# A gated cross-attention stack on one core: first key weights requested first, context rounded in three pieces, GpSimd's power behind the first weight rounding, keys of batch 1 last

## The chip, the cores and the metric

The kernel runs on 1 core of one Trainium2 chip. The metric is device time in microseconds, median over the runs. The profiled execution is a single one; its span runs from its first to its last instruction.

## What is computed

Four layers of a gated cross-attention model on x (2 x 256 x 512) with a context (2 x 512 x 512). Each layer adds a gated attention and a gated MLP to x, each behind a layer norm. The change is in the opening of the first attention, which is, cut to what matters:

```
def _L0_xattn_ref(latents, context, Wq, Wk, Wv, Wo):      # 32 heads, 4 key/value heads, head dim 128
    hidden_states = jnp.concatenate([context, latents], axis=1)
    q = (latents @ Wq).reshape(b, q_len, N_KV_HEADS, N_GROUPS, HEAD_DIM)
    k = (hidden_states @ Wk).reshape(b, kv_len, N_KV_HEADS, HEAD_DIM)
    v = (hidden_states @ Wv).reshape(b, kv_len, N_KV_HEADS, HEAD_DIM)
    scores = jnp.einsum('bqhgd,bkhd->bhgqk', q, k) * scale
    attn = jax.nn.softmax(scores.astype(jnp.float32), axis=-1).astype(q.dtype)
    out = jnp.einsum('bhgqk,bkhd->bqhgd', attn, v)
    return out.reshape(b, q_len, N_HEADS * HEAD_DIM) @ Wo

x = x + jnp.tanh(g_xattn[0]) * _L0_xattn_ref(_layernorm(x, axis=-1), ctx_4096, ...)
x = x + jnp.tanh(g_ffn[0]) * _L0_ffn_ref(_layernorm(x, axis=-1), ...)
...                                                       # layers 1 to 3 alike
```

## The kernel before

Each engine runs a program of its own, written out by hand, and waits on semaphores. Nothing is scheduled at run time: what stands first on an engine runs first.

**Products in three parts.** To multiply in float32 accuracy, every operand is kept as a rounded part (HI) and the rest (LO), and each product is three passes: HI by HI, HI by LO, LO by HI (`PAIRS`). So a weight or a context tile can be used only when both parts exist. Weights are split by GpSimd in `att_pool` (L526 writes HI, L529 writes LO). The context, 512 rows by 1024 columns in `ctxraw`, is split by ScalarE (HI, L1899) and VectorE (LO, L1934), one batch (4 x 512 columns per partition) at a time; `ctx_split` counts the finished pieces. The transposed latents `xT` are split out of PSUM by ScalarE (L419) and VectorE (L425).

**The jobs.** The attention's small products are jobs. ("K", u, c) projects the keys of key head u: c = 0 and 1 are the context of batch 0 and 1, c = 2 the latents of both. ("Q", h, 0) projects a head's queries, ("V", u, c) six tiles of values, ("O", h, r) the output rows. A K or Q job is 12 matmuls of 512 columns (L560, L583). Below, K0, K1, K2 and Q0 mean the four jobs of `self.first`. ScalarE and VectorE take every job's result out of PSUM in the order of `place`, and scores(n) (L614) is the first step of the main loop: 128 items of scores, softmax, transpose and weighted values, with jobs between them. TensorE is in order, so that whatever delays scores(0) delays all behind it.

**The opening, before.** SyncE requests, in this order: the context of batch 0 (1 MB), x (1 MB), the context of batch 1 (1 MB), the gates, the key weights (256 KB), and then the stream of `att_sp`: the weights of query heads 0 and 1 and, behind the latter, the MLP's `worg`, `fwq`, `fkeys` (`mlp0_early_sp`). From the third entry on, the stream's request j waits for the split of entry j - 2. GpSimd splits the key weights and both query weights, and then computes rstd as a power of the variances (`ln_first_pool`, L382). VectorE has by then taken the statistics (L340 to L345) and waits for rstd to write the normalised rows (L348); TensorE transposes them (L399).

The place of `ctxraw` in memory overlaps the output weights before the change (its group begins with a filler `kept0` of 12 x 512 words), so GpSimd waits for the second context split before it goes on to the value weights.

Of the kernel before, what the change touches and what calls it, by code (L numbers as in the profile page):

```python
# [15 lines left out]
F32 = mybir.dt.float32  # L16
# [53 lines left out]
class Attention:  # L70
# [7 lines left out]
    def __init__(self, tag, heads, kv, hd, tiles, first_tile, before):  # L78
        self.tag, self.heads, self.kv, self.hd = tag, heads, kv, hd
        self.g = heads // kv  # L80
        self.items = RT * heads
        self.pairs = self.items // 2
        self.scale = float(hd) ** -0.5
        inner, last = {}, {}
        for h in range(heads):
            n = RT * h
            if h + 1 < heads:
                last[n + 1] = ("Q", h + 1, 0)
            last[n + 6], last[n + 7], last[n + 8], inner[n + 9] = [("O", h, r) for r in range(RT)]
        for u in range(1, kv):  # L90
            n = RT * self.g * u
            inner[n - 2], inner[n - 1], inner[n] = ("K", u, 0), ("K", u, 2), ("K", u, 1)
        for u in range(0, kv, 2):
            n, v, h = RT * self.g * u, [("V", u, c) for c in range(6)], self.g * u - 1
            if u == 0:
                last[0], inner[2], last[2], inner[3], last[3], inner[4] = v
            else:
                inner[n + 2], last[n + 2], inner[n + 3], inner[n + 4], last[n + 4], inner[n + 5] = v
                last[n + 3], inner[n + 6], last[n + 6], inner[n + 7] = [("O", h, r) for r in range(RT)]
                last[n + 7], inner[n + 8], last[n + 8], inner[n + 9] = [("O", h + 1, r) for r in range(RT)]  # L100

        self.tail = [("O", heads - 1, 2), ("O", heads - 1, 3)]
        for at in (inner, last):
            for n in [n for n, job in at.items() if job in self.tail]:
                del at[n]
        self.steps = [(n, inner.get(n), last.get(n)) for n in range(self.items + 4)]
        self.first = [("K", 0, 0), ("K", 0, 1), ("K", 0, 2), ("Q", 0, 0)]
        order = self.first + [j for _, *both in self.steps for j in both if j] + self.tail
        self.place = {j: i + 1 for i, j in enumerate(order)}
        assert len(self.place) == len(order) == 3 * kv + 3 * kv + heads + RT * heads  # L110
        self.bank = {j: 7 for j in order}
        for c in range(3):
            self.bank["K", 0, c] = c
        for c in (0, 1, 3):
            self.bank["V", 0, c] = 6
        self.bank[self.tail[0]], self.bank[self.tail[1]] = 3, 6
        self.free, used = {}, {}
        for j in order[3:-2]:
            self.free[j] = used.get(self.bank[j], 0)
            used[self.bank[j]] = self.place[j]  # L120
        self.hi_place = {j: i + 1 for i, j in enumerate(j for j in order if j[0] != "O")}


        need = [(RT * h - 3, 0, ("q", h, 0)) for h in range(heads)] + [(RT * h + 6, 1, ("o", h, 0)) for h in range(heads)]
        need += [(RT * self.g * u - 3, 1, ("k", u, 0)) for u in range(kv)]
        need += [(RT * self.g * u + 2, p, ("v", u, p)) for u in range(0, kv, 2) for p in range(2)]
        self.stream = [e for *_, e in sorted(need)]
        a, b = self.stream.index(("k", 0, 0)), self.stream.index(("q", 0, 0))
        self.stream[a], self.stream[b] = self.stream[b], self.stream[a]
        self.split = {e: i + 1 for i, e in enumerate(self.stream)}  # L130

        self.amax_at, self.scale_at, self.step_at, self.load_before, self.round_after, self.store_before = (
            {} for _ in range(6))
        for i, h in enumerate(tiles):
            n = first_tile + i
            self.amax_at[RT * h + 1], self.scale_at[RT * h + 5], self.step_at[RT * h + 9] = n, n, n
            self.load_before["q", h + 2, 0], self.round_after["o", h + 2, 0], self.store_before["o", h + 4, 0] = n, n, n
        self.stored = first_tile + len(tiles)

        J, E = len(order), len(self.stream)  # L140
        count = {"raw0": 8 * E, "raw1": 8 * E, "split_hi": E, "split": E, "w_full": J, "w": J,
                 "w_hi": len(self.hi_place), "rden": heads}
        count.update({n: self.items for n in ("scores", "nmax", "exps", "turned", "pT_hi", "pT")})
        count.update({n: self.pairs for n in ("pv", "oT_hi", "oT")})
        self.before = before.after if before else dict.fromkeys(count, 0)
        self.after = {n: self.before[n] + count[n] for n in count}
# [6 lines left out]
def build(nc, t, out):  # L153
    with ExitStack() as ctx:
# [75 lines left out]
            values_of = {A0: vv0, A1: vv1}  # L230

        with ExitStack() as grp:
            sb("kept0", [P, 12, 512], F32, grp)
            ctxraw = sb("ctxraw", [P, KT, B * CTX], F32, grp)


# [76 lines left out]
        with ExitStack() as grp:  # L313
# [6 lines left out]
            x8 = sb("x8", [P, D], F8, grp)  # L320
            hq = sb("hq", [P, 2, FPAD], BF16, grp)
            hqT = sb("hqT", [P, FT, P], BF16, grp)

        block = ctx.enter_context(nc.Block())

# [118 lines left out]
        def att_sp(sp, A, u, between=None):  # L444
# [18 lines left out]
            for j, entry in enumerate(A.stream):  # L463
# [12 lines left out]
                else:  # L476
                    att_wait(sp, A, "split", 0)
                to, arrived = raw[:, j % 2, :], sem(f"att_raw{j % 2}")
                if w == "k":
                    sp.dma_start(to[:, 0:KT * A.hd], t[f"{A.tag}_wk"][h]).then_inc(arrived, 16)  # L480
                elif w == "v":
                    n = KT * A.hd
# [11 lines left out]
        def att_pool(g, A, layer_norm):  # L494
# [15 lines left out]
            for j, entry in enumerate(A.stream):  # L510
# [23 lines left out]
                    att2_split_pool(g, l2wkv, l2wkv_raw, "l2_wkv", 1)  # L534
                if A is A1 and entry == ("o", 13, 0):
                    att2_split_pool(g, l2wq, l2wq_raw, "l2_wq", 2)
                if j == 2:
                    layer_norm()

        def values_tile(A, part, pair, c):  # L540
# [4 lines left out]
        def att_pe(pe, A, u):  # L545
# [6 lines left out]
            def job(what):  # L552
                kind, h, c = what
                b = A.bank[what]
                if kind == "K":
                    wait("split", A.split["k", h, 0])
                    for k in range(KT):
                        for wp, xp in PAIRS:
                            rhs = ctxT[:, xp, k, c * CTX:(c + 1) * CTX] if c < B else xT[:, xp, k, :]
                            last = nc.tensor.matmul(bank(b, 512, hd), wk[:, wp, k * hd:(k + 1) * hd], rhs,  # L560
# [39 lines left out]
            def scores(n):  # L600
# [2 lines left out]
                if r == 0:  # L603
                    wait("w", A.place["Q", h, 0])
                if n % (RT * A.g) == 0:
                    wait("w", A.place["K", group, 2])
                if n % (RT * A.g) == 2:
                    wait("w", A.place["K", group, 1])
                if n >= 2:
# [35 lines left out]
                    last.then_inc(sem("att_pv"), 1)  # L645

            if A is A0:
                pe.wait_ge(sem("ctx_split"), 1)
                job(A.first[0])
                turn_pe(pe, u)  # L650
                pe.wait_ge(sem("ctx_split"), 2)
                job(A.first[1])
            else:
                job(A.first[0])
                job(A.first[1])
                turn_pe(pe, u)
            pe.wait_ge(sem("xT_lo"), (u // 2 + 1) * RT)
            job(A.first[2])
            job(A.first[3])
            for n, inner, end in A.steps:  # L660
                if n < A.items:
                    scores(n)
# [1173 lines left out]
        @block.sync  # L1836
        def _(sp):
            context = t["ctxT"].rearrange("(k p) n -> p k n", p=P)
            sp.dma_start(ctxraw[:, :, 0:CTX], context[:, :, 0:CTX]).then_inc(sem("ctx_loaded0"), 16)
            sp.dma_start(x[:], t["x"].rearrange("(r p) d -> p r d", p=P)).then_inc(sem("x_loaded"), 16)  # L1840
            sp.dma_start(ctxraw[:, :, CTX:B * CTX], context[:, :, CTX:B * CTX]).then_inc(sem("ctx_loaded1"), 16)
# [15 lines left out]
        def _(g):  # L1857
# [3 lines left out]
            g.wait_ge(sem("const"), 3)  # L1861
            nc.gpsimd.affine_select(out=ident[:], in_=ident[:], compare_op=ALU.not_equal, fill=1.0, base=0,
                                    pattern=[[-1, P]], channel_multiplier=1).then_inc(sem("const"), 1)
            def before_output_weights():
                ln_first_pool(g)
                g.wait_ge(sem("ctx_split"), 2)

            att_pool(g, A0, before_output_weights)
            ln_pool(g, 1)
            mlp0_pool(g)  # L1870
            att_pool(g, A1, lambda: ln_pool(g, 2))
# [22 lines left out]

        @block.scalar
        def _(a):
            for b in range(B):
                a.wait_ge(sem(f"ctx_loaded{b}"), 16)
                nc.scalar.activation(ctxT[:, HI, :, b * CTX:(b + 1) * CTX], ctxraw[:, :, b * CTX:(b + 1) * CTX],  # L1899
                                     ACT.Copy).then_inc(sem("ctx_hi"), 1)  # L1900
            a.wait_ge(sem("gates_loaded"), 16)
            nc.scalar.activation(tg[:], gates[:], ACT.Tanh).then_inc(sem("gates_ready"), 1)
            turn_act(a, 0)
            att_act(a, A0, 0)
            a.wait_ge(sem("w3_stored"), 32 * A0.stored)
            turn_act(a, 1, plain=True)
# [21 lines left out]

        @block.vector
        def _(v):  # L1930
            def split_context(b):
                cols = slice(b * CTX, (b + 1) * CTX)
                v.wait_ge(sem("ctx_hi"), b + 1)
                nc.vector.tensor_tensor(ctxT[:, LO, :, cols], ctxraw[:, :, cols], ctxT[:, HI, :, cols].bitcast(F32),  # L1934
                                        ALU.subtract).then_inc(sem("ctx_split"), 1)

            split_context(0)
            ln_first_dve(v)
            split_context(1)
            turn_dve(v, 0)  # L1940
            v.wait_ge(sem("gates_ready"), 1)
            v.wait_ge(sem("ctx_split"), 2)
            att_dve(v, A0, 0)
            mlp0_dve(v)
            turn_dve(v, 2)
# [95 lines left out]
```

## Time and profile before

| | |
|---|---|
| median of 3 runs | 1447.77 us (1447.07 to 1454.72) |
| profiled execution, device time | 1453.91 us |
| its span | 1452.2 us |
| TensorE busy | 1362.6 us, 94% of the span |
| VectorE, ScalarE, GpSimd busy | 945.3, 588.6, 475.1 us |
| mean granted TensorE clock | 0.969 |

Device time is 1.71 us more than the span. In the page's slices all but the first show TensorE at seven tenths busy or more; the first slice, 36 us long, shows it at four tenths. Idle time of an engine that nobody waits for costs nothing. The granted clock is 1.00 at 2.4 GHz and 0.50 at 1.2 GHz.

### The profile page before, as it was taken

The page shows a single profiled execution, that of the slowest core. Times are in us where ns is not written, and L with a number is a line of the kernel's source. Part 1 is how long each engine was busy: PE and PEld are TensorE (multiplying, and loading weights), DVE is VectorE, ACT ScalarE, POOL GpSimd, SP SyncE. Part 2 cuts the span into 40 slices and gives each one's busy share as a digit, 9 for nine tenths or more (in the row PEclk, how much of TensorE's full clock was granted, in tenths as well). Part 3 has the DMA queues.
Part 4 walks back from the last instruction along what each step waited for, and adds up shares of the span by engine and source line. Part 5 has one row for each costly group of instructions (what it writes and reads, how often), then busy time and mean ns, then how long its engine had stood idle before and what let it go on. Part 6 is the DMA issues. An engine that isn't in the chain of part 4 may idle for free.

```text
span 1452.2 us, 21125 instructions
## 1 busy us (share of the span) xinstructions
PE 1362.6 (94%) x8219; PEld 1081.1 (74%) x8219; DVE 945.3 (65%) x1375; ACT 588.6 (41%) x1012; POOL 475.1 (33%) x359
## 2 busy tenths in 40 slices
PE   4999999999999999989999999999899999899766
PEld 3989889988889889964788888888774444577422
DVE  4488778864688688762466864767656673352596
ACT  2444444443344344430244443444344677222112
POOL 4226435361235525411321671235213002144100
PEclk9999999999999999999999999999997899999888
DMA  5111111021012111011111111002012000461000
GB/s 174 51 53 47 52 47 60 26 70 37 23 52 77 34 51 48 19 47 39 55 33 38 39 37 41 28 17 67 1 50 77 1 1 1 143 168 44 1 1 29
DMA packets 54337, 68.19 MB, mean 47 GB/s; under 512 B 26416, under 2 KB 34896, under 8 KB 54240
## 3 DMA queue, kind: packets, MB, share of 16 engines
q1 hardware_dynamic: 54240, 66.84, 15.3%
q8 instruction: 67, 1.10, 0.3%
q14 instruction: 30, 0.25, 0.1%
HBM read 57.13 MB, written 5.37 MB: 43 GB/s over the span
## 4 chain that ended last, share of the span: by engine, by line
PE 84%; DVE 9%; ACT 3%; issue 2%; DMA 1%; POOL 0%; SPq 0%; POOLq 0%; ACTq 0%; DVEq 0%
PE ps L639 13%; PE ps L614 12%; PE ps L590 9%; PE ps L623 9%; PE ps L583 8%; PE ps L575 5%; PE ps L560 5%; PE ps L1496 4%; PE ps L1124 3%; PE ps L1150 3%; PE ps L1509 2%; PE ps L1106 1%; PE ps L1135 1%; PE ps L862 1%; PE ps L869 1%
## 5 line engine op out<-in xcount | busy, mean ns | idle before, releaser
L708 ACT ACTIVATE pT<-ps 128x768 fp32r<-128x768 f32 x192 | 156.0, 812 | 288.7 <-PE ps L623 287.1
L639 PE MATMUL ps<-pT,vv 128*128 128x256 f32 (+1 forms) x1728 | 251.3, 290 | 2.5 <-DVE oT L818 2.5
L811 DVE TENSOR_TENSOR pT<-ps,pT 128x768 fp32r<-128x768 f32 x192 | 183.7, 957 | 77.9 <-ACT pT L708 77.2
L614 PE MATMUL ps<-kT,qT 128*128 128x512 f32 (+3 forms) x1152 | 231.6, 336 | 2.8 <-DVE qT L763 2.8
L614 PEld LDWEIGHTS ps<-kT,qT 128*128 128x128 f32 (+1 forms) x1152 | 201.5, 188 | 43.9 <-DVE qT L763 3.7
L639 PEld LDWEIGHTS ps<-pT,vv 128*128 128x128 f32 (+1 forms) x1728 | 215.1, 180 | 3.1 <-DVE pT L811 2.9
L716 ACT ACTIVATE prob<-ps,rows_and_turned 128x768 f32<-128x768 f32 x192 | 172.2, 897 | 84.9 <-DVE rows_and_turned L799 84.9
L799 DVE TENSOR_REDUCE rows_and_turned<-ps 128x1 f32<-128x768 f32 x192 | 182.7, 952 | 26.0 <-PE ps L614 25.7
L526 POOL TENSOR_TENSOR wo<-raw,one 128x512 fp32r<-128x512 f32 (+1 forms) x48 | 49.9, 1040 | 395.1 <-PE ps L590 394.6
L590 PE MATMUL ps<-wo,oT 128*128 128x512 f32 (+1 forms) x576 | 169.6, 403 | 5.6 <-DVE qT L763 2.6
L623 PE MATMUL ps<-ident,prob 128*128 128x128 f32 x1152 | 157.1, 272 | 0.4 <-DVE pT L811 0.4
L753 DVE SCALAR_TENSOR_TENSOR x<-ps,rows_and_turned,x 128x512 f32<-128x512 f32 x192 | 143.1, 745 | 7.2 <-PE ps L590 7.2
L583 PE MATMUL ps<-xT,wq 128*128 128x512 f32 (+1 forms) x576 | 142.2, 395 | 0.0
L623 PEld LDWEIGHTS ps<-ident,prob 128*128 128x128 f32 x1152 | 132.3, 140 | 11.0 <-ACT prob L716 1.3
L583 PEld LDWEIGHTS ps<-xT,wq 128*128 128x128 f32 (+1 forms) x576 | 100.2, 179 | 26.3
L590 PEld LDWEIGHTS ps<-wo,oT 128*128 128x128 f32 (+1 forms) x576 | 94.9, 189 | 18.7 <-DVE qT L763 4.4
L1340 DVE TENSOR_REDUCE qrow<-ps 128x1 f32<-128x512 f32 x128 | 83.3, 687 | 38.1 <-PE ps L1124 37.0
L1436 POOL TENSOR_TENSOR f2w<-f2raw,f2w 128x1024 fp32r<-128x1024 f32 (+1 forms) x22 | 43.1, 1964 | 182.8 <-ACT f2w L1540 181.7
L526 POOL TENSOR_TENSOR wq<-raw,one 128x512 fp32r<-128x512 f32 (+1 forms) x48 | 46.9, 976 | 106.9 <-PE ps L583 103.5
L1306 ACT ACTIVATE prob<-ps 128x1024 f32<-128x1024 f32 x64 | 65.4, 1025 | 29.0 <-PE ps L1135 28.7
L560 PE MATMUL ps<-ctxT,wk 128*128 128x512 f32 (+1 forms) x192 | 50.5, 414 | 18.4 <-POOL wk L529 15.2
L387 POOL TENSOR_TENSOR rstd<-vare,neghalf 128x1 f32<-128x1 f32 x28 | 20.9, 746 | 139.1 <-DVE vare L364 139.1
(227 smaller groups left out, 1908.5 us busy)
## 6 DMA issues: line engine op xcount, KB each, us to landing
f2raw<-in_f_w SPq DMA_DIRECT2D x11, 776.0 KB, 4.9
rows_and_turned<-in_m_w SPq DMA_DIRECT2D x11, 768.0 KB, 4.2
raw<-in_l_wq SPq DMA_DIRECT2D x32, 256.0 KB, 2.7
raw<-in_l_wo SPq DMA_DIRECT2D x32, 256.0 KB, 2.7
raw<-in_l_wq SPq DMA_DIRECT2D x16, 192.0 KB, 2.4
raw<-in_l_wo SPq DMA_DIRECT2D x16, 192.0 KB, 2.5
w3gu<-rows_and_turned SPq DMA_DIRECT2D x11, 256.0 KB, 3.2
ctxraw<-in_ctxT SPq DMA_DIRECT2D x2, 1024.0 KB, 7.5
```

The lines of the kernel that those rows point to most:

```text
L526: nc.gpsimd.tensor_tensor(dst[:, HI], src, one[0:src.shape[0], :].to_broadcast(src.shape), ALU.mult).then_inc(sem("att_split_hi"), 1)
L560: last = nc.tensor.matmul(bank(b, 512, hd), wk[:, wp, k * hd:(k + 1) * hd], rhs, start=(k == 0 and (wp, xp) == PAIRS[0]), stop=(k == KT - ...
L583: last = nc.tensor.matmul(bank(b, 512, hd), wq[:, h % 2, wp, k * hd:(k + 1) * hd], xT[:, xp, k, :], start=(k == 0 and (wp, xp) == PAIRS[0] ...
L590: last = nc.tensor.matmul(bank(b), oT[0:hd, h % 2, op, c * P:(c + 1) * P], wo[0:hd, h % 2, wp, :], start=(op, wp) == PAIRS[0], stop=(op, w ...
L614: last = nc.tensor.matmul(sc[:, lo:hi], qT[0:hd, h % 2, qp, r * P:(r + 1) * P], kT[0:hd, kp, b, lo:hi], start=(qp, kp) == PAIRS[0], stop=( ...
L623: last = nc.tensor.transpose(ps[:, 4 + j // 3, (j % 3) * P:(j % 3 + 1) * P], prob[:, m % 3, j * P:(j + 1) * P], ident[:])
L639: last = nc.tensor.matmul(bank(6, 256, hd), vv[:, vp, b * VT + j, group % 2 * hd:(group % 2 + 1) * hd], pT[:, q % 2, pp, j, :], start=(j = ...
L708: nc.scalar.activation(turned_p(m, HI), ps[:, 4:6, 0:S // 2].rearrange("p a (j c) -> p a j c", j=3), ACT.Copy).then_inc(sem("att_pT_hi"), 1)
L716: nc.scalar.activation(prob[:, n % 3, :], sc[:, 0:S], ACT.Exp, bias=nmax[:, n % 32:n % 32 + 1], accum_out=rsum[:, n % 32:n % 32 + 1]).then ...
L753: nc.vector.scalar_tensor_tensor(x[:, c, :], bank(A.bank[what]), rden[:, n:n + 1], x[:, c, :], ALU.mult, ALU.add).then_inc(sem("att_w"), 1)
L799: nc.vector.tensor_reduce(nmax[:, n % 32:n % 32 + 1], sc[:, 0:S], AX.X, ALU.max, negate=True).then_inc(sem("att_nmax"), 1)
L811: nc.vector.tensor_tensor(turned_p(m, LO), ps[:, 4:6, 0:S // 2].rearrange("p a (j c) -> p a j c", j=3), turned_p(m, HI).bitcast(F32), ALU. ...
```

## The change

SyncE requests the key weights ahead of everything. The context is split in three pieces: the first half of batch 0's contraction rows, its second half, and all of batch 1. VectorE splits the third piece behind the split of `xT`, ScalarE's tanh of the gates goes behind its part of `xT`. GpSimd computes rstd directly behind the split of the key weights. TensorE runs K0 (its first half needs the first piece alone), the transposes, K2, Q0, and last K1. `ctxraw` moves up in memory, clear of the output weights.

```diff
         self.first = [("K", 0, 0), ("K", 0, 1), ("K", 0, 2), ("Q", 0, 0)]
+        if before is None:
+            self.first = [("K", 0, 0), ("K", 0, 2), ("Q", 0, 0), ("K", 0, 1)]
...
+        if before is None:
+            self.bank["K", 0, 1] = 5
...
-            sb("kept0", [P, 12, 512], F32, grp)
+            sb("kept0", [P, 31, 512], F32, grp)
...
+        CTX_PARTS = ((0, 0, 2), (0, 2, KT), (1, 0, KT))
...
-                if w == "k":
+                if A is A0 and j == 0:
+                    pass
+                elif w == "k":
...
-                if j == 2:
+                if j == (0 if A is A0 else 2):
                     layer_norm()
...
                     for k in range(KT):
+                        if what == ("K", 0, 0) and A is A0 and k % 2 == 0:
+                            pe.wait_ge(sem("ctx_split"), k // 2 + 1)
...
-                    wait("w", A.place["K", group, 2])
+                    wait("w", max(A.place["K", group, 2], A.place["Q", h, 0]))
...
             if A is A0:
-                pe.wait_ge(sem("ctx_split"), 1)
                 job(A.first[0])
                 turn_pe(pe, u)
-                pe.wait_ge(sem("ctx_split"), 2)
+                pe.wait_ge(sem("xT_lo"), RT)
                 job(A.first[1])
+                job(A.first[2])
+                pe.wait_ge(sem("ctx_split"), 3)
+                job(A.first[3])
...
+            sp.dma_start(raw[:, 0, :], t["l0_wk"][0]).then_inc(sem("att_raw0"), 16)
             sp.dma_start(ctxraw[:, :, 0:CTX], context[:, :, 0:CTX]).then_inc(sem("ctx_loaded0"), 16)
...
-            def before_output_weights():
-                ln_first_pool(g)
-                g.wait_ge(sem("ctx_split"), 2)
-
-            att_pool(g, A0, before_output_weights)
+            att_pool(g, A0, lambda: ln_first_pool(g))
...
-            for b in range(B):
+            for b, lo, hi in CTX_PARTS:
...
+            turn_act(a, 0)
             a.wait_ge(sem("gates_loaded"), 16)
             nc.scalar.activation(tg[:], gates[:], ACT.Tanh).then_inc(sem("gates_ready"), 1)
-            turn_act(a, 0)
...
             split_context(0)
+            split_context(1)
             ln_first_dve(v)
-            split_context(1)
             turn_dve(v, 0)
+            split_context(2)
             v.wait_ge(sem("gates_ready"), 1)
```

GpSimd's first instructions behind its constants, before (wk, wq, wv are the weights of keys, queries and values, raw what was loaded, rstd the power):

```order
L526 TENSOR_TENSOR wk<-raw,one 128x512
L529 TENSOR_TENSOR wk<-raw,wk 128x512
L526 TENSOR_TENSOR wq<-raw,one 128x512
L529 TENSOR_TENSOR wq<-raw,wq 128x512
L526 TENSOR_TENSOR wq<-raw,one 128x512
L529 TENSOR_TENSOR wq<-raw,wq 128x512
L382 TENSOR_TENSOR rstd<-vare,neghalf 128x4
L526 TENSOR_TENSOR wv<-raw,one 128x512
```

The same place on GpSimd after the change:

```order
L534 TENSOR_TENSOR wk<-raw,one 128x512
L537 TENSOR_TENSOR wk<-raw,wk 128x512
L388 TENSOR_TENSOR rstd<-vare,neghalf 128x4
L534 TENSOR_TENSOR wq<-raw,one 128x512
L537 TENSOR_TENSOR wq<-raw,wq 128x512
L534 TENSOR_TENSOR wq<-raw,one 128x512
L537 TENSOR_TENSOR wq<-raw,wq 128x512
L534 TENSOR_TENSOR wv<-raw,one 128x512
```

The power moved ahead of the four instructions that split the query weights of heads 0 and 1, so these four now stand directly behind it.

TensorE's first instructions, before:

```order
L560 MATMUL ps<-ctxT,wk 128x512 x12
L399 MATMUL ps<-ident,rows_and_turned 128x128 x16
L560 MATMUL ps<-ctxT,wk 128x512 x12
L560 MATMUL ps<-xT,wk 128x512 x12
L583 MATMUL ps<-xT,wq 128x512 x12
L614 MATMUL ps<-kT,qT 128x512 x3
```

TensorE's first instructions after the change:

```order
L570 MATMUL ps<-ctxT,wk 128x512 x12
L405 MATMUL ps<-ident,rows_and_turned 128x128 x16
L570 MATMUL ps<-xT,wk 128x512 x12
L593 MATMUL ps<-xT,wq 128x512 x12
L570 MATMUL ps<-ctxT,wk 128x512 x12
L624 MATMUL ps<-kT,qT 128x512 x3
```

The second job on the context (K1) moved from directly behind the transposes to directly ahead of the scores; the number of matmuls is the same.

## Rows read from the trace of the kernel before

**Rows 1.** The page: span, and TensorE's busy time.

```profile
span 1452.2 us, 21125 instructions
PE 1362.6 (94%) x8219; PEld 1081.1 (74%) x8219; DVE 945.3 (65%) x1375; ACT 588.6 (41%) x1012; POOL 475.1 (33%) x359
```

**Rows 2.** Timeline, 0 to 38 us: start, us, engine, line [idle before, releaser].

```profile
5.95 1.91 ACT L1899 ACTIVATE ctxT<-ctxraw 128x2048 fp32r<-128x2048 f32 x1 [3.87 <-DMA ctxraw<-in_ctxT]
7.89 2.29 DVE L1934 TENSOR_TENSOR ctxT<-ctxraw,ctxT 128x2048 fp32r<-128x2048 f32 x1 [7.89 <-ACT ctxT L1899]
10.10 2.47 DVE L340 BATCH_NORM_STATS2 stat<-x 128x6 f32<-128x512 f32 x4
...
13.02 0.77 DVE L345 TENSOR_SCALAR vare<-mv 128x4 f32<-128x4 f32 x1
...
13.84 1.26 POOL L529 TENSOR_TENSOR wk<-raw,wk 128x512 fp32r<-128x512 f32 x1
...
15.25 4.85 PE L560 MATMUL ps<-ctxT,wk 128*128 128x512 f32 x12 [15.25 <-POOL wk L529]
...
20.26 1.03 POOL L382 TENSOR_TENSOR rstd<-vare,neghalf 128x4 f32<-128x4 f32 x1
21.32 1.92 DVE L348 TENSOR_SCALAR rows_and_turned<-x,mv,rstd 128x512 f32<-128x512 f32 x4 [7.54 <-POOL rstd L382]
...
22.02 3.06 PE L399 MATMUL ps<-ident,rows_and_turned 128*128 128x128 f32 x16 [1.92 <-DVE rows_and_turned L348]
...
25.11 0.60 ACT L419 ACTIVATE xT<-ps 128x512 fp32r<-128x512 f32 x1 [0.26 <-PE ps L399]
25.35 2.48 DVE L425 TENSOR_TENSOR xT<-ps,xT 128x512 fp32r<-128x512 f32 x4
...
25.49 3.29 PE L560 MATMUL ps<-ctxT,wk 128*128 128x512 f32 x12 [0.41 <-DVE ctxT L1934]
...
28.62 2.96 PE L560 MATMUL ps<-xT,wk 128*128 128x512 f32 x12
...
31.42 2.96 PE L583 MATMUL ps<-xT,wq 128*128 128x512 f32 x12
...
35.79 1.32 PE L614 MATMUL ps<-kT,qT 128*128 128x512 f32 x6 [1.41 <-DVE qT L763]
```

**Rows 3.** Tiles ctxraw and x, time from request to landing; DMA in one microsecond.

```profile
DMA to landing us min/median/max: 5.1/7.5/9.9
...
DMA to landing us min/median/max: 7.8/7.8/7.8
...
7.00:8.00 1.00, 0.00 (x0) 1.00 1.02 399
```

**Rows 4.** Timeline at 695 us, second attention's layer norm: GpSimd and VectorE.

```profile
695.59 0.78 POOL L387 TENSOR_TENSOR rstd<-vare,neghalf 128x1 f32<-128x1 f32 x1 [2.79 <-DVE vare L364]
696.34 0.82 POOL L526 TENSOR_TENSOR wv<-raw,one 128x384 fp32r<-128x384 f32 x1
696.40 1.04 DVE L368 TENSOR_SCALAR rows_and_turned<-x,mv,rstd 128x512 f32<-128x512 f32 x1 [0.44 <-POOL rstd L387]
```

**Rows 5.** Timeline at 88 us, first attention: GpSimd and VectorE.

```profile
87.57 1.04 POOL L526 TENSOR_TENSOR wq<-raw,one 128x512 fp32r<-128x512 f32 x1 [2.11 <-PE ps L583]
...
88.69 0.19 DVE L773 TENSOR_SCALAR rows_and_turned<-rows_and_turned 128x48 uint32<-128x48 uint32 x1
88.69 1.33 POOL L529 TENSOR_TENSOR wq<-raw,wq 128x512 fp32r<-128x512 f32 x1
88.79 1.28 DVE L775 TENSOR_SCALAR rows_and_turned<-rows_and_turned 128x48 uint32<-128x48 uint32 x1
```

**Rows 6.** Windows of all engines; the clock granted to TensorE stands behind POOL's.

```profile
23.00:25.50 2.50, 2.08 (x11) 1.68 (x9) 2.50 (x3) 1.86 (x4) 0.00 (x0) 0.50 0.00 0
...
26.50:34.00 7.50, 7.50 (x34) 5.99 (x33) 3.32 (x6) 1.20 (x2) 3.64 (x4) 1.00 0.27 70
1104.50:1135.50 31.00, 30.86 (x143) 12.80 (x142) 16.49 (x26) 15.11 (x18) 6.59 (x2) 0.50 0.00 1
```

More of the change, by code:

```diff
@@ L656, in att_pe @@
                 turn_pe(pe, u)
-            pe.wait_ge(sem("xT_lo"), (u // 2 + 1) * RT)
-            job(A.first[2])
-            job(A.first[3])
+                pe.wait_ge(sem("xT_lo"), 2 * RT)
+                job(A.first[2])
+                job(A.first[3])
             for n, inner, end in A.steps:
@@ L1896, in _ @@
         def _(a):
-            for b in range(B):
+            for b, lo, hi in CTX_PARTS:
                 a.wait_ge(sem(f"ctx_loaded{b}"), 16)
-                nc.scalar.activation(ctxT[:, HI, :, b * CTX:(b + 1) * CTX], ctxraw[:, :, b * CTX:(b + 1) * CTX],
+                nc.scalar.activation(ctxT[:, HI, lo:hi, b * CTX:(b + 1) * CTX], ctxraw[:, lo:hi, b * CTX:(b + 1) * CTX],
                                      ACT.Copy).then_inc(sem("ctx_hi"), 1)
+            turn_act(a, 0)
             a.wait_ge(sem("gates_loaded"), 16)
             nc.scalar.activation(tg[:], gates[:], ACT.Tanh).then_inc(sem("gates_ready"), 1)
-            turn_act(a, 0)
             att_act(a, A0, 0)
@@ L1930, in _, with split_context @@
         def _(v):
-            def split_context(b):
+            def split_context(i):
+                b, lo, hi = CTX_PARTS[i]
                 cols = slice(b * CTX, (b + 1) * CTX)
-                v.wait_ge(sem("ctx_hi"), b + 1)
-                nc.vector.tensor_tensor(ctxT[:, LO, :, cols], ctxraw[:, :, cols], ctxT[:, HI, :, cols].bitcast(F32),
+                v.wait_ge(sem("ctx_hi"), i + 1)
+                nc.vector.tensor_tensor(ctxT[:, LO, lo:hi, cols], ctxraw[:, lo:hi, cols],
+                                        ctxT[:, HI, lo:hi, cols].bitcast(F32),
                                         ALU.subtract).then_inc(sem("ctx_split"), 1)
             split_context(0)
+            split_context(1)
             ln_first_dve(v)
-            split_context(1)
             turn_dve(v, 0)
+            split_context(2)
             v.wait_ge(sem("gates_ready"), 1)
-            v.wait_ge(sem("ctx_split"), 2)
             att_dve(v, A0, 0)
```

## The prediction, made before the changed kernel ran

> **What bounds the kernel now.** I read the page first: TensorE is busy 94% of the span [rows 1], and every item of the first attention hangs on its in-order queue. The opening is the one long exception, so the timeline of the first 38 us comes next [rows 2]. Up to scores(0) at 35.79, TensorE does five blocks and waits four times: 15.25 us for the key weights, 1.92 for the normalised rows, 0.41 for the second context split, 1.41 for Q0's rounding. Its work is 15.25 to 20.1 (K0), 22.02 to 25.08 (transposes), and three jobs from 25.49, which start 3.13, 2.80 apart. Behind scores(0) everything is the same code in the same order, so what the change is worth is the move of scores(0): the program before and the program after must be compared at that one instruction.
>
> Three chains end there. The key weights are the last of the opening's large loads; GpSimd has them split at 15.10. The variances are ready at 13.79 (13.02 + 0.77), but GpSimd, in order, has two query weights to split first and takes the power only at 20.26, so the rows start at 21.32 and not at about 14.9. And K1 stands ahead of K2 and Q0, with Q0's rounding bare behind it (1.41).
>
> **The change part by part.**
>
> *Loads.* The key weights go first: 256 KB at the 399 GB/s of the queue [rows 3] push each load behind them back by 0.66 us. The context of batch 0 landed 5.1 us after its request at 0.81, so now at 6.6; x landed 7.8 after 1.32, so now at 9.8; batch 1 at 12.4 instead of 11.8. The key weights themselves land by about 3.5 and are split (1.04 + 1.26, and two gaps) by 6.0, well before anyone asks.
>
> *Context in pieces.* ScalarE takes 1.91 for 2048 columns and 0.60 for 512 [rows 2], so by a straight line 1.04 for 1024; VectorE 2.29 for 2048 and 0.62 for 512 (2.48 / 4), so 1.18. HI is done at 7.65 and 8.7, LO at 8.9 and 10.1. VectorE's statistics start at 10.1, as before (10.10), behind x at 9.8. The variances stay at 13.79: this part moves K0 from 15.25 to about 9.0, and K0 (4.85) is done at 13.9, before any row exists. So K0's 6 us gain is not on the path: the next late thing is the rows.
>
> *The power.* It starts at 13.86 instead of 20.26, ends at 14.89, and the first row can start at 14.92 instead of 21.32: 6.40 earlier. This is the largest term.
>
> *What now stands behind the power.* Before, GpSimd idled while VectorE wrote the four rows, since it waited for the second context split. Now four weight splits follow the power at once. The trace has that situation: at 695.59 a power is followed by a weight split at 696.34, and VectorE's row, started at 696.40, takes 1.04 instead of 0.54 and ends 0.28 after GpSimd's instruction does [rows 4]. With 128 x 512 weights the hold is 1.04. Does each of the four rows wait, or only the first? At 88 us, VectorE has short instructions in a row [rows 5]: the one at 88.69 slips in (0.19) between two GpSimd instructions, the next, at 88.79, asks for no semaphore and still takes 1.28, until GpSimd's 1.33 are over. They take turns. So I let every row wait for one GpSimd instruction: HI of head 0 ends at 15.90 and row 0 at 16.2; LO (1.33) ends at 17.3, row 1 at 17.6; HI of head 1 at 18.45, row 2 at 18.7; LO at 19.85, row 3 at 20.1. Unhindered, row 3 would end at 16.84. This costs 3.3 us. Bounds: nothing, if the rows got ahead of GpSimd each time, and 1.0 if only the first waits; I take the full 3.3, because both places in the trace show the wait and the second shows it repeated.
>
> The Trainium skill, in "SBUF — State Buffer", section "Who interferes with whom", has VectorE and GpSimd share a port pair that one instruction holds to its end, and says "Issue order, not op shape, decides who blocks". If the rows were issued first each time, the sum below would gain the 3.3 again; by the trace, where GpSimd's next instruction starts 0.03 before the power's recorded end, it would not.
>
> *From the last row to K2.* The last row's transposes follow by 0.15 and take up to 0.77 (3.06 / 4), ScalarE's part 0.03 + 0.60, VectorE's 0.04 + 0.62: `xT` is complete at 22.4. VectorE's third context split is now behind this and no longer in it. K2 starts at 22.4; before, K1 started at 25.49.
>
> *The clock.* TensorE has pauses of 2.4 us ahead of the transposes, about half a microsecond after each row, and 1.3 ahead of K2. Before, a pause of 1.9 was followed by a stretch at 1.2 GHz, in which the whole window from 23.0 to 25.5 lies [rows 6]; the transposes took 3.06 and K1 had its first half microsecond at that level. K0, the first work after a long idle time, took 4.85 where a job at full clock takes 2.96. So K2 may cost from nothing extra to, with Q0 partly slow too, 2.8 more. I take one whole slow job, 4.85 - 2.96 = 1.9.
>
> *The three jobs.* K2, Q0, K1 start 2.8 apart at full clock: 22.4 + 1.9 + 3 x 2.8 = 32.7. Q0's rounding (bare 1.41 before) lies beside K1, which covers it; without that cover it would cost 1.41. The third context split on VectorE (2.29, and it may wait its turn with GpSimd, up to 1.3 more) is done by about 26, and K1 needs it at 29.9: free, with nearly 4 us of cover. K0's LO then waits behind it on VectorE, needed only at scores(0). ScalarE's tanh (moved) is first needed by the value job. On SyncE, the query weights of head 1 and the MLP's 1.25 MB are requested from 6 us on, so the value weights land at 20 to 23 and are split by 27; their job comes at 34.
>
> *Sum.* scores(0) moves from 35.79 to 32.75: 3.0 us. Span 1452.2 - 3.0 = 1449.2, plus the 1.7 outside it, 1450.9 for an execution like the profiled one. That one is 6.1 above the median, with nothing in the opening to tell why, so I take the 3.0 off the median: 1444.7.
>
> **The rivals.**
>
> *The rows are not held back* (or only the first). For it: the four rows are queued and ready, and the two places show at most two waits in a row. Against: both places show VectorE waiting. `xT` is complete at 19.2 to 20.2 and the gain is 3.0 + 2.3 to 3.3, and with the faster transposes less of the clock's 1.9 too: 5.3 to 7.8, so 1440 to 1442.5. Chance 0.20.
>
> *The loads take it back.* The requests for query head 1 and `worg` (1 MB) now come at 6 us, with x and batch 1 still in flight. If they share instead of queueing, x lands up to 2.6 us later (1 MB at 399 GB/s), variances and power with it, and 0.4 is left: 1447.4, no change. Against: before, the 256 KB of the key weights were the last to land though requested early enough to share. Here also belongs any wait that I have not seen of 2 to 4 us. Chance 0.17.
>
> *Slower, by the clock.* In this place the mechanism is that short bursts with pauses leave TensorE at 1.2 GHz, and the dense work behind does not raise it soon. The price is 4.85 - 2.80 = 2.05 per job's worth of work. Without any clock cost the gain is 4.9, so it is gone after 2.4 slow jobs, 12 us, and slower by 0.5% needs 5.9 jobs, some 29 us at the low level: 1455. The trace has such a stretch, 31 us at 0.50 with TensorE busy throughout, in the third attention [rows 6]. Against: it has far fewer instructions per microsecond than this place, and the jobs from 26.5 to 34 run at 1.00. Chance 0.04.
>
> **How the numbers follow.** The likeliest case, rows and GpSimd in turns with some slow clock, gets 0.57: gain 2.1 (2.8 lost to the clock) to 4.9 (nothing lost), 1442.9 to 1445.7. The remaining 0.02 are for what I have no name for. About 0.5% (7.2 us) is what a measurement of this kernel can tell from no change, and half of it lies between single runs already (1447.07 to 1454.72). The range takes in the rival of free rows at its likely end and the one of the loads with a microsecond for the median: 1440.5 to 1448.5. Faster by over 0.5% needs free rows and a kind clock, or a spread between medians that adds to either: 0.14. Slower by over 0.5%: 0.04. Within: 0.82.
>
> **What the profile would show.** Right: K0 at about 9.0 and 0.40 us a matmul; stats still at 10.1; power at 13.9; four rows that take 1.2 to 1.4 us each and interleave with GpSimd's splits until about 20; `xT` complete at 22.4; K1 directly ahead of scores(0) at about 32.7, with no idle time between; granted clock 0.50 in part of 16 to 26. Wrong: rows of 0.54 that end at 16.9; x landing later than 10; scores(0) waiting for VectorE; value jobs that wait for GpSimd; or a difference behind scores(0) that the opening does not explain.

## The result and the profile after

The changed kernel took 1445.06 us, the median of 22 runs (1442.9 to 1452.45), against 1449.23 for the kernel before in 22 runs (1447.07 to 1460.13). The ratio is 0.9962, with a 95% interval from 0.9948 to 0.9976: 0.38% or 5.5 us faster, within the 0.5% band, though the lower end of the interval lies past it. The two medians are 4.2 us apart; the 5.5 are the ratio's. The forecast was 1444.7, no change beyond 0.5%.

The page of the profiled execution, which took 1442.9 us, beside [rows 1]:

```profile
span 1441.2 us, 21119 instructions
PE 1358.8 (94%) x8213; PEld 1080.7 (75%) x8219; DVE 948.0 (66%) x1376; ACT 589.0 (41%) x1013; POOL 478.0 (33%) x359
```

The timeline of its opening answers to [rows 2] (start, us, engine, line, then idle time and releaser; lines 346, 351, 354, 388, 431, 534, 537, 570, 624 and 1944 are the 340, 345, 348, 382, 425, 526, 529, 560, 614 and 1934 of before):

```profile
3.74 1.04 POOL L534 TENSOR_TENSOR wk<-raw,one 128x512 fp32r<-128x512 f32 x1 [2.13 <-DMA raw<-in_l_wk]
...
8.87 5.32 PE L570 MATMUL ps<-ctxT,wk 128*128 128x512 f32 x12 [8.87 <-DVE ctxT L1944]
9.78 2.47 DVE L346 BATCH_NORM_STATS2 stat<-x 128x6 f32<-128x512 f32 x4
...
12.69 0.17 DVE L351 TENSOR_SCALAR vare<-mv 128x4 f32<-128x4 f32 x1
12.94 1.03 POOL L388 TENSOR_TENSOR rstd<-vare,neghalf 128x4 f32<-128x4 f32 x1 [6.82 <-DVE vare L351]
14.00 4.31 DVE L354 TENSOR_SCALAR rows_and_turned<-x,mv,rstd 128x512 f32<-128x512 f32 x4 [1.14 <-POOL rstd L388]
14.19 1.26 POOL L534 TENSOR_TENSOR wq<-raw,one 128x512 fp32r<-128x512 f32 x1 [0.22 <-DMA raw<-in_l_wq]
...
15.52 1.33 POOL L537 TENSOR_TENSOR wq<-raw,wq 128x512 fp32r<-128x512 f32 x1
...
16.82 1.22 POOL L534 TENSOR_TENSOR wq<-raw,one 128x512 fp32r<-128x512 f32 x1
...
18.24 2.61 DVE L431 TENSOR_TENSOR xT<-ps,xT 128x512 fp32r<-128x512 f32 x4
...
20.90 4.52 PE L570 MATMUL ps<-xT,wk 128*128 128x512 f32 x12 [1.41 <-DVE xT L431]
...
28.06 2.92 PE L570 MATMUL ps<-ctxT,wk 128*128 128x512 f32 x12
...
30.82 1.20 PE L624 MATMUL ps<-kT,qT 128*128 128x512 f32 x6
```

The reader is to see three things. The power starts at 12.94 instead of 20.26. The four rows behind it take 4.31 us instead of 1.92. And scores(0) starts at 30.82 instead of 35.79, 4.97 earlier, with no idle time ahead of it. That accounts for the 5.5 us of the runs within their interval (3.5 to 7.5).

The spans of the two profiled executions differ by 11.0 us. The other 6.0 are behind scores(0): 1416.4 from there to the end before, 1410.4 after. That is no work of the change, since a second profiled execution of the changed kernel, with a span of 1448.6, has 1416.3 there. The granted clock goes with it: in the stretch around 1100 us its mean was 0.58 before and 0.77 after, in the same part of the program, and 0.58 again (181 matmuls from 1099 to 1136) in the second execution.

```profile
1099.00:1135.50 36.50, 35.54 (x161) 0.58 0.00 0
```

```profile
1099.00:1136.00 37.00, 36.55 (x233) 0.77 0.00 1
```

(Windows of TensorE, the first of the kernel before, the second of the changed one: length, busy time and matmuls, granted clock, DMA.) In 37 us the changed kernel's execution did 233 matmuls there, the other 161 in 36.5. The opening is also not the only place where TensorE is less busy: the last two slices of the page of before, 36 us each, stand at six tenths. They have no part in this change.

### The profile page after: what moved, and what is told of

Its sections match the earlier page's. It is cut to its first block, busy times and chain, and to the rows that moved or that the text cites. A ratio compares the mean times of both kernels' runs of the same rounds, so it can differ in the third digit from the quotient of the medians.

```text
span 1441.2 us, 21119 instructions
## 1 busy us (share of the span) xinstructions
PE 1358.8 (94%) x8213; PEld 1080.7 (75%) x8219; DVE 948.0 (66%) x1376; ACT 589.0 (41%) x1013; POOL 478.0 (33%) x359
## 4 chain that ended last, share of the span: by engine, by line
PE 84%; DVE 11%; ACT 3%; issue 2%; DMA 0%; POOL 0%; POOLq 0%; ACTq 0%; SPq 0%; DVEq 0%
PE ps L649 13%; PE ps L624 12%; PE ps L600 9%; PE ps L633 9%; PE ps L593 8%; PE ps L570 5%; PE ps L585 5%; PE ps L1508 4%; PE ps L1136 3%; PE ps L1162 3%; PE ps L1521 2%; PE ps L1118 1%; PE ps L1147 1%; PE ps L874 1%; PE ps L881 1%
## 5 line engine op out<-in xcount | busy, mean ns | idle before, releaser
L534 POOL TENSOR_TENSOR wo<-raw,one 128x512 fp32r<-128x512 f32 (+1 forms) x48 | 50.0, 1042 | 395.1 <-PE ps L600 394.7
L534 POOL TENSOR_TENSOR wq<-raw,one 128x512 fp32r<-128x512 f32 (+1 forms) x48 | 47.3, 986 | 105.4 <-PE ps L593 102.3
L714 ACT ACTIVATE qT<-ps 128x512 fp32r<-128x512 f32 (+1 forms) x48 | 28.7, 598 | 90.1 <-PE ps L593 90.1
```

The costliest lines, as they stand in the source:

```text
L534: nc.gpsimd.tensor_tensor(dst[:, HI], src, one[0:src.shape[0], :].to_broadcast(src.shape), ALU.mult).then_inc(sem("att_split_hi"), 1)
```

## The experiments

The measure is the start of scores(0) in one profiled execution. The changed kernel profiled twice had 30.82 and 32.33, so that a difference under 1.5 us is read only together with its rows. Of the other kernels, all but the one with the power alone moved were profiled once. Expectations name theories and rivals as they stood before each run.

| kernel | scores(0) starts | four rows take | first job behind the transposes (K2 or K1) takes |
|---|---|---|---|
| before | 35.79 | 1.92 | 3.29 |
| changed | 30.82 and 32.33 | 4.31 and 5.26 | 4.52 and 4.78 |
| rows first | 27.15 | 1.92 | 3.07 |
| half splits | 28.61 | 3.32 | 3.06 |
| kept warm | 29.29 | 4.32 | 3.06 |
| two pieces | 31.10 | 5.25 | 3.06 |
| keys requested late | 32.23 | 5.27 | 3.06 |
| K1 second | 35.31 | 5.31 | 5.49 |
| power late | 38.62 | 5.25 | 5.49 |
| before, power alone moved | 30.93, 31.62, 32.41 | 1.92 | 3.01, 2.98, 3.01 |
| before, keys' request alone moved | 34.89 | 1.91 | 3.92 |

**1. GpSimd waits until the rows are written.**

```diff
-            att_pool(g, A0, lambda: ln_first_pool(g))
+            def before_queries():
+                ln_first_pool(g)
+                g.wait_ge(sem("rows_ready"), RT)
+            att_pool(g, A0, before_queries)
```

> One edit on the changed kernel: GpSimd, behind the power, waits until VectorE has written all four rows, and only then splits the query weights. My theory (the two take turns at a shared resource, one GpSimd instruction per row): the rows take 1.9 us again instead of 4.31, xT is complete 2.4 us earlier (about 18.5), scores(0) starts at 30.8 - 2.4 = 28.4, or up to 1.5 earlier still if K2 meets a full clock. Rival A (the rows were slow for a reason of their own, GpSimd is not it): rows stay at 4.3, scores(0) at 30.8. Rival B (the query weights then come too late): Q0 waits for its split, which is done at about 16 + 2.4 = 18.4; that is ahead of Q0's turn at 21 to 23, so I expect no wait.

Timeline of its opening, VectorE, GpSimd and TensorE:

```profile
14.18 1.92 DVE L354 TENSOR_SCALAR rows_and_turned<-x,mv,rstd 128x512 f32<-128x512 f32 x4 [1.14 <-POOL rstd L388]
14.87 1.94 PE L405 MATMUL ps<-ident,rows_and_turned 128*128 128x128 f32 x16 [1.50 <-DVE rows_and_turned L354]
...
16.17 1.04 POOL L534 TENSOR_TENSOR wq<-raw,one 128x512 fp32r<-128x512 f32 x1 [2.03 <-DVE rows_and_turned L354]
...
18.70 3.07 PE L570 MATMUL ps<-xT,wk 128*128 128x512 f32 x12 [1.90 <-DVE xT L431]
21.61 2.96 PE L593 MATMUL ps<-xT,wq 128*128 128x512 f32 x12
...
27.15 1.20 PE L624 MATMUL ps<-kT,qT 128*128 128x512 f32 x6
```

The rows take 1.92 again, the transposes follow in one block, K2 meets the full clock, and scores(0) comes 3.67 earlier than in the changed kernel, 8.64 earlier than before. Rival A falls; rival B too, since Q0 follows K2 without idle time. The runs agree: 1445.14 us, 12 runs, against 1453.55 for the kernel before beside it (17 runs), a ratio of 0.9942 (0.9919 to 0.9966). By the rows this is the version to keep; it was not timed beside the changed kernel, and the interval overlaps that of the changed kernel (0.9948 to 0.9976).

**2. Half as long splits.** The HI and LO instructions of the first two query weights become two of 256 columns each (L534 and L537, `parts = 2 if A is A0 and j in (1, 2) else 1`); the work is the same.

```diff
+                for i in range(parts):
+                    s = src[:, i * m:(i + 1) * m]
+                    op = nc.gpsimd.tensor_tensor(dst[:, HI, i * m:(i + 1) * m], s,
+                                                 one[0:s.shape[0], :].to_broadcast(s.shape), ALU.mult)
```

> The changed kernel with the four weight splits behind the power cut into two instructions of 256 columns each, the same work. Theory (a row waits for one GpSimd instruction, whatever it is, and not for an amount of GpSimd work): rows 1 to 3 wait about 0.65 each instead of 1.1 to 1.3, so the four rows take about 3.2 instead of 4.31, and scores(0) comes at least 1.0 earlier, 29.8 or below (to 28.3 if K2 then runs at full clock). Rival (a row waits until GpSimd has nothing queued, or for a whole weight): the rows take 4.3 or more, and scores(0) is at 30.8 or later.

```profile
14.39 3.32 DVE L354 TENSOR_SCALAR rows_and_turned<-x,mv,rstd 128x512 f32<-128x512 f32 x4 [1.14 <-POOL rstd L388]
17.63 2.47 DVE L431 TENSOR_TENSOR xT<-ps,xT 128x512 fp32r<-128x512 f32 x4
20.02 2.36 DVE L1952 TENSOR_TENSOR ctxT<-ctxraw,ctxT 128x2048 fp32r<-128x2048 f32 x1
```

```profile
14.32 1.37 POOL L538 TENSOR_TENSOR wq<-raw,one 128x256 fp32r<-128x256 f32 x2
```

```profile
15.36 1.32 PE L405 MATMUL ps<-ident,rows_and_turned 128*128 128x128 f32 x8 [1.79 <-DVE rows_and_turned L354]
```

(Timelines of VectorE, GpSimd and TensorE.) 3.32 for the four rows, 3.2 expected: a row waits for one GpSimd instruction, however short, and then gets its turn ahead of the next. The rival falls. That 3.2 was met is in part luck: it was set for three waiting rows, from the 4.31. Here GpSimd's first half (14.32) started ahead of row 0 (14.39), whose transposes began only at 15.36, so all four waited. The like comparison is the changed kernel's second execution, 5.26: 1.31 us a row with whole splits, 0.83 with half ones.

**3. TensorE kept busy in the pauses.** Extra transposes of the identity, read by nobody.

```diff
                 job(A.first[0])
-                turn_pe(pe, u)
+                keep_warm(3)
+                for r in range(RT):
+                    turn_row(pe, u, r)
+                    keep_warm(3 if r < RT - 1 else 8)
```

> The changed kernel with extra transposes of the identity on TensorE, whose result nobody reads, in its pauses: 3 behind K0, 3 behind each of the first three rows, 8 behind the last. Theory (1.5 us of the changed kernel's opening are the low clock in K2, which the pauses between held-back rows bring): the rows still take over 4 us, K2 takes about 3.0 instead of 4.52 and scores(0) comes at about 29.3. Rival (the level at K2 is not set by what TensorE does between the rows): K2 stays at 4 us or more and scores(0) at 30.8 or later.

Windows of TensorE (busy time and matmuls, granted clock behind), first the changed kernel, then this one:

```profile
14.00:17.00 3.00, 1.47 (x9) 1.00 1.00 360
17.00:20.50 3.50, 2.17 (x8) 0.54 0.31 101
20.50:23.50 3.00, 2.60 (x6) 0.50 0.36 104
```

```profile
14.00:17.00 3.00, 2.54 (x18) 1.00 1.01 369
17.00:20.50 3.50, 2.52 (x19) 1.00 0.33 102
20.50:23.50 3.00, 2.68 (x12) 1.00 0.26 86
```

The rows were held back as in the changed kernel (4.32), the clock stayed at 1.00, K2 took 3.06, and scores(0) came at 29.29, where 29.3 was expected. So the changed kernel's opening pays 1.5 us for the clock alone. Of the 3.67 us that experiment 1 gives back, 1.5 are this and the rest is the rows' wait. The size of the price is shown; that the pauses bring it is not. K2 also took 3.06 or 3.07 in experiments 1 and 2, with pauses of 1.50 to 1.90 us left as they were, and in experiment 7, whose pauses add up to more than the changed kernel's. The rival, that TensorE's work between the rows does not set the level, still stands.

**4. The power late**, behind both query weights (`if j == 2:` for both attentions).

> The changed kernel with GpSimd's power behind the split of the second query weights, where it stood before. Theory (the power's place is the largest term, and turns with GpSimd add to it): power at about 19 instead of 12.9, rows from 20, again 1.2 to 1.4 us each because the value weights' splits follow, if these have landed (19.3); xT complete at about 26.5 and scores(0) at 36 to 37, so that the remaining edits together are worth nothing or less than nothing against 35.8 of before. Rival (the context pieces and the order of the jobs carry the gain): scores(0) below 34.

scores(0) at 38.62, later than before, and later than the 36 to 37 that I expected. The power came at 18.55; the rows waited four times, for the value weights' splits; and this time the clock was at 1.2 GHz from 16.4 to 33.5, so that K2 took 5.49 and Q0 3.31. Without the power's new place the other edits are a loss of 2.8 us in this execution, and the two slow jobs are as much (2.43 and 0.35 more than the 3.06 and 2.96 of experiment 3). With these at full clock the other edits would be worth about nothing.

**5. K1 second**, as before, with VectorE's split of batch 1 ahead of its part of `xT`.

```diff
-            self.first = [("K", 0, 0), ("K", 0, 2), ("Q", 0, 0), ("K", 0, 1)]
+            self.first = [("K", 0, 0), ("K", 0, 1), ("K", 0, 2), ("Q", 0, 0)]
...
+            split_context(2)
             turn_dve(v, 0)
-            split_context(2)
```

> The changed kernel with the jobs in their old order (K0, K1, K2, Q0) and VectorE's split of batch 1 back ahead of its part of xT. Theory: scores(0) is 1.4 us later for Q0's rounding, which is bare again, and up to 1.5 more where the context split holds up K1 and xT; so 32.2 to 33.7. Rival (K1's place is worth nothing, since TensorE does the same four jobs): 30.8.

```profile
22.57 5.49 PE L568 MATMUL ps<-ctxT,wk 128*128 128x512 f32 x12 [1.93 <-DVE ctxT L1942]
27.86 3.15 PE L568 MATMUL ps<-xT,wk 128*128 128x512 f32 x12
...
35.31 1.29 PE L622 MATMUL ps<-kT,qT 128*128 128x512 f32 x6 [1.50 <-DVE qT L773]
```

(Timeline, TensorE.) 35.31, 1.6 beyond my upper end. The rows took 5.31 here, so the fair comparison is the changed kernel's second execution (5.26, scores(0) at 32.33): 3.0 later, of which 1.50 are Q0's bare rounding, 0.7 a slower first job (5.49 against 4.78), 0.4 its later start, and 0.4 the slower start of the second job and what is left.

**6. The key weights requested late.**

> The changed kernel with the key weights requested behind the gates, as before; everything else changed. Theory: they land at 12.7, are split by 15.1, and the power, which stands behind the split, starts at 15.2 instead of 12.9; rows and GpSimd take turns as in the changed kernel, so scores(0) comes 2.3 later, at about 33.1. A side question: VectorE's variance instruction took 0.77 before and 0.17 after the change; if GpSimd's key split held it up before, it takes over 0.5 here again. Rival (K0 has 5 us to spare, so the weights' place is worth nothing): 30.8.

32.23 where 33.1 was expected: the power started 1.95 later (14.89), all four rows waited, but K0 now ran until 20.1, the transposes followed in one block, and K2 took 3.06 at full clock. Against the changed kernel's second execution, where all four rows waited too (32.33), requesting the key weights late costs nothing: the later rows and the cheaper K2 cancel. The side question stays unanswered by this run, since the variances came at 12.18, ahead of GpSimd's 12.55.

**7. Two pieces instead of three.**

> The changed kernel with the context split in two pieces (a batch each) instead of three. Theory (K0 is done before the rows exist, so starting it earlier is worth nothing): K0 starts about 1.1 later, at 10.0, and ends at about 14.9 instead of 14.2, some 0.2 after the first row is ready, so scores(0) stays within 0.4 of 30.8. Rival (the three pieces are on the path): scores(0) 1.1 later, 31.9.

```profile
16.34 0.63 PE L405 MATMUL ps<-ident,rows_and_turned 128*128 128x128 f32 x4 [0.93 <-DVE rows_and_turned L354]
...
17.66 0.66 PE L405 MATMUL ps<-ident,rows_and_turned 128*128 128x128 f32 x4 [0.69 <-DVE rows_and_turned L354]
...
18.84 0.66 PE L405 MATMUL ps<-ident,rows_and_turned 128*128 128x128 f32 x4 [0.53 <-DVE rows_and_turned L354]
...
20.25 0.66 PE L405 MATMUL ps<-ident,rows_and_turned 128*128 128x128 f32 x4 [0.75 <-DVE rows_and_turned L354]
...
22.64 3.06 PE L570 MATMUL ps<-xT,wk 128*128 128x512 f32 x12 [1.73 <-DVE xT L431]
```

(Timeline, TensorE.) 31.10, inside the expected 0.4, but for another reason. K0 started 2.1 later, not 1.1, and the statistics 0.93 later (10.71), because VectorE has to finish the whole batch first; all four rows waited and `xT` was complete 1.7 later, of which 0.93 are the statistics and the rest is mainly row 0's wait. K2 ran in 3.06, and the clock paid that back. Why it stayed at 1.00 is open: from 17.0 to 20.5 TensorE was busy for 1.57 us here and kept it, while the changed kernel's clock fell at 17.3, after 1.58 busy us from 14.0 on. The pieces are on the path, through VectorE's queue and not through K0; they were worth nothing only net of the clock, and against the changed kernel's second execution (32.33) the kernel with two pieces is even 1.2 earlier.

**8. Single parts on the kernel before.** The power alone (`if j == (0 if A is A0 else 2):` with the old callback, so that GpSimd also waits there for the second context split), and the key weights' request alone.

> The kernel before with one line changed: GpSimd computes the power, and then waits for the second context split, directly behind the key weights' split instead of behind the second query weights'. Theory: the power starts at 15.1 instead of 20.26; the rows take 1.9, since GpSimd waits for the context split and holds nobody back; the transposes follow K0 at 20.1 without a pause; K1, K2, Q0 and Q0's bare rounding put scores(0) at about 32.1, 3.7 earlier than before. Rival (the query weights, now split from 20.4 to 25.1, come late for Q0 at 27.7): no, unless the loads are late too. Rival B (the power's place alone is worth little): above 35.

> The kernel before with only the key weights' request moved ahead of all others. Theory: K0 starts at about 10.8, behind the context's LO, but the power still stands behind both query weights, the first of which lands at about 13.9: power at about 18.6, rows at 19.6, so scores(0) at 34 to 34.5, later by up to a microsecond more if the 5 us pause of TensorE ahead of the rows lowers the clock for K1. Rival (the weights' early landing carries the gain): below 32.

```profile
12.50 1.04 POOL L526 TENSOR_TENSOR wk<-raw,one 128x512 fp32r<-128x512 f32 x1 [10.89 <-DMA raw<-in_l_wk]
12.71 0.38 DVE L343 BATCH_NORM_AGGREGATE mv<-stat 128x2 f32<-128x6 f32 x4
13.12 0.44 DVE L345 TENSOR_SCALAR vare<-mv 128x4 f32<-128x4 f32 x1
...
15.90 1.92 DVE L348 TENSOR_SCALAR rows_and_turned<-x,mv,rstd 128x512 f32<-128x512 f32 x4 [2.33 <-POOL rstd L382]
...
19.24 1.91 PE L399 MATMUL ps<-ident,rows_and_turned 128*128 128x128 f32 x16
...
30.93 1.32 PE L614 MATMUL ps<-kT,qT 128*128 128x512 f32 x6 [1.41 <-DVE qT L763]
```

(Timeline of the first.) This one line puts scores(0) at 30.93, where 32.1 was expected and the whole change has 30.82: the old wait keeps GpSimd out of the rows' way, and K0, late, leaves TensorE no pause. In two more executions it came at 31.62 and 32.41, so the two kernels spread over the same 1.5 us. The key weights alone give 0.90 us (34.89, 0.4 beyond the upper end of the expectation), with the rival refuted.

So is the one line as fast as the whole change? Timed twice:

> The kernel before with the power, and the wait for the context split, behind the key weights' split, once more and timed. It had scores(0) at 30.93, the changed kernel 30.82; so by the opening alone it should be faster than the kernel before by 4.9 us, a ratio of about 0.9966, not to be told from the changed kernel's 0.9962. Rival (the other edits are worth something behind scores(0)): a ratio of 0.998 or more.

> The one-line kernel (power and wait behind the key weights' split) once more. Its first timed set gave a ratio of 0.9998 although scores(0) came 4.2 us earlier; eight of its twelve executions had a mean granted clock below 0.970. Theory (that was the clock's chance): the ratio is now within 0.001 of the changed kernel's beside it, 0.996 to 0.998. Rival (the one-line kernel draws the lower clock more often, or the other edits are worth something behind scores(0)): again 0.999 or more, while the changed kernel has 0.996 to 0.9975.

> The changed kernel once more, beside the next kernel on the same chip. Its scores(0) came 4.97 us earlier than in the kernel before; ratio expected 0.996 to 0.9975 against the kernel before, if the tail behind scores(0) is as it was but for the granted clock.

The first set gave 0.9998 (0.9978 to 1.0018), which is the rival's figure; its interval lies just above the one that the changed kernel had on another chip (0.9948 to 0.9976). The second gave 0.9974 (0.9947 to 1.0001), beside 0.9966 (0.9943 to 0.9989) for the changed kernel on the same chip. On one chip the intervals overlap and decide nothing between the two. The mean granted clock goes with most of the spread: among the executions at 0.973 to 0.976, a cut chosen after the fact, the medians are 1448.8 for the kernel before (25 of them), 1445.0 for the changed kernel (17), 1444.4 for the one line (9) and 1440.2 for rows first (4), in line with their scores(0). At 0.970 or less the one line had 14 of its 24 executions, rows first 7 of 12, the changed kernel 14 of 34, the kernel before 25 of 57. Whether its place in time makes the one-line kernel draw the lower clock more often, or that is chance, stays open.

## Why the prediction was right, step by step

- **The power, the largest term (6.40).** Right; 7.32 measured (20.26 to 12.94), and the one-line kernel shows that its place is worth as much as all edits together.
- **The variances.** I kept them at 13.79; they came at 12.86. 0.32 of that is VectorE's earlier start on the pieces (9.78 against 10.10). The other 0.60 was a mis-sized row: the 0.77 of the variance instruction [rows 2] was itself a wait for GpSimd, which ran the key weights' HI from 12.72 to 13.76, while the instruction ended at 13.79. In the one-line kernel it shows again: in the first execution it took 0.44 and ended at 13.56, GpSimd's at 13.54; in the third 0.69, to 13.84, GpSimd's at 13.82. In the second it began at 12.80, 0.01 ahead of GpSimd's, and took 0.17, as it did where GpSimd was idle. The change removed a wait that I had found elsewhere and not looked for here.
- **The rows and GpSimd in turns (3.3).** Right. In the second execution the rows took 5.26, 3.3 more than 1.92:

```profile
14.33 5.26 DVE L354 TENSOR_SCALAR rows_and_turned<-x,mv,rstd 128x512 f32<-128x512 f32 x4 [1.14 <-POOL rstd L388]
```

```profile
14.26 1.05 POOL L534 TENSOR_TENSOR wq<-raw,one 128x512 fp32r<-128x512 f32 x1
```

  (Timelines of VectorE and GpSimd.) In the first they took 4.31: the query weights landed 0.22 after GpSimd had asked, so row 0 got through before them and only three rows waited. Experiments 1 and 2 show the mechanism and its unit. The Trainium skill's sentence in "SBUF — State Buffer", "Who interferes with whom", that issue order decides, agrees with both executions; by their rows, the order hangs on when one 256 KB load lands.
- **From the last row to K2.** 2.3 forecast (20.1 to 22.4, though its terms add up to 2.21), 2.6 measured in both executions. The last row's transposes, at the low clock, took 1.12 in both where 0.77 was allowed.
- **The clock (1.9).** Right in kind; K2 at 4.52 instead of 3.06 is 1.5, and the low level lasted from 17.3 to 24.1. But the 1.9 rested on the wrong rows. It was K0's 4.85 less 2.96, and the view of that stretch of the kernel before has the clock at 1.00 (behind POOL's busy time):

```profile
15.00:20.00 5.00, 4.75 (x12) 3.57 (x12) 0.00 (x0) 0.00 (x0) 4.39 (x5) 1.00 0.70 252
```

  So K0's time does not price the low level, and no run shows why it takes 4.3 to 5.5 us at 1.00. A job that lies wholly at 0.50 took 5.49 (experiments 4 and 5), 2.4 more than 3.06. One whole slow job would have been 2.4; that K2 was slow for part of its time only brought the measured term near the forecast.
- **K0 off the path, and Q0's rounding under K1.** The second right: no idle time ahead of scores(0), and 1.50 comes back in experiment 5. The first is right as far as K0's end goes, which does not set the rows. Whether an early K0, by the idle time behind it, also lowers the clock for K2 is not shown: K2 was fast with a late K0 (experiments 6 and 7), but also with K0 at 9.04 and 9.26 (experiments 1 and 2).
- **The sum.** scores(0) at 32.75 forecast; 30.82 and 32.33 measured. The gain in device time was 5.5 where 3.0 was forecast. The 1.9 of the first execution are the variances (0.9), row 0's luck (about 0.9) and a cheaper clock term (0.4), less 0.3 behind the rows. The median of before on record was 1447.77 from 3 runs, and 1449.23 from 22. This start, 1.5 too low, and a gain forecast too small cancel, so that the absolute figure came out within 0.4: that closeness is luck. One of the forecast's own signs of being wrong appeared too, a difference behind scores(0) that the opening does not explain (6.0 us between the two profiles); the second execution puts it down to the clock.
- **The rivals and the band.** Free rows: experiment 1 makes them true, and scores(0) then comes 8.64 earlier than before, above the 5.3 to 7.8 given, by the variances' 0.9. Loads that share: nothing of it; the statistics started at 9.78 and ScalarE had batch 1 at 12.28, as queueing gives. A clock that stays low: not in this kernel, but experiment 4 had 17 us of it and ended slower than before. The argument against it was misread: the slow stretch has 143 matmuls in 31 us and the full-clock one 34 in 7.5 [rows 6], 4.6 and 4.5 a microsecond, which is not far fewer. And the three single runs on record spread over 7.65 us, which is all of the 7.2 and not half.

## What to carry to other kernels

When an instruction is moved forward on an in-order queue, look at what then stands directly behind it: here the power's new place let four weight splits collide with the very instructions that waited for the power, and one more wait, which looks like a loss, added three quarters (3.67 us) to what the change had won (4.97). A duration in the old trace can be a wait in disguise; before it goes into a sum, compare it with other instructions of its kind and with what a neighbouring engine did at that time. And the clock can take back what an earlier start wins: 1.5 us here. What in TensorE's work brings the low level is open after these runs, so compare several executions before an edit is credited or blamed for it.

## What was not expected of the hardware

Short VectorE instructions suffer as much as long ones: the variance of 4 columns took 0.17 alone, 0.44 and 0.77 beside GpSimd. The wait goes both ways, in whole instructions: in the changed kernel VectorE's third context split took 3.27 instead of 2.29, and GpSimd's instruction beside it 2.85 instead of 1.04.

```profile
20.76 3.27 DVE L1944 TENSOR_TENSOR ctxT<-ctxraw,ctxT 128x2048 fp32r<-128x2048 f32 x1
...
22.09 2.85 POOL L534 TENSOR_TENSOR wv<-raw,one 128x512 fp32r<-128x512 f32 x1 [0.20 <-DMA raw<-in_l_wv]
```

(Timeline of the changed kernel.) And two executions of the changed kernel differ by 5.9 us behind scores(0), where the clock is all that I found to tell them apart: more than the change is worth by the ratio.
